# x1's product into the down accumulator moved to unit 26 of the attention, and the scaling of x1's rows moved from VectorE to ScalarE

## The chip, the cores and the metric

The kernel runs on one core of one Trainium2 chip. A core has TensorE (PE, matrix products into PSUM), VectorE (DVE), ScalarE (ACT), GpSimd (POOL) and SyncE (SP, which issues DMAs). The metric is the device time of one execution in microseconds.

## The reference, cut to what matters

```python
xn  = _layernorm(x)                        # x is (8, 512, 128): eight batch rows
s   = attention_1(xn, Wq, Wk, Wv, Wo, ...) # causal, weights 1 - tanh(energy)^2
h   = rmsnorm(xn, norm1_w)
ctx = softmax_attention(h @ wq, h @ wk, h @ wv)
X   = xn + ctx @ wo                        # x1 in the kernel
h2  = rmsnorm(X, norm2_w)
combine = top-2 of 8 experts by softmax(h2 @ router_w)
moe = swiglu(h2, shared) + sum_e combine[:, e] * swiglu(h2, expert e)
out = x + s * silu(X + moe)
```

`X + moe` is the sum that one PSUM accumulator collects: nine down products (the shared expert and eight routed ones) and x1 itself.

## The kernel before, in words

The eight batch rows are done one after another by an order written out by hand, and `row(u, it, following)` stands in each engine's program for one of them. Engines meet at counting semaphores alone, and each engine works strictly through its own program, so whatever stands behind a wait on an engine stands still with it. A row takes about 131 us. It has three parts.

**Units 0 to 15** (N1 = 16) are the softmax attention of the feed-forward block: TensorE makes scores into the PSUM tiles S0 and S1 (L1112), ScalarE takes their exponential into a slot of the tile PT (`weights`, L613), and TensorE multiplies it with V (`with_v`, L1139). VectorE spends most of this part on maxima over score blocks of 512 columns (`maximum`, L758).

**Units 16 to 27** are the second attention. ScalarE writes a sigmoid (L613 again), and VectorE turns it into weights (`weigh`, L813, two halves for each unit). Beside the units stand named pieces of work, given by the table PLACES: at 23 "proj2", behind which VectorE adds the projection to x1 (L857); at 25 "Q1", which ScalarE copies out of PSUM twice (`projection`, L572 and L573); at 26 "h2T", the transpose of the scaled rows (L1048 on TensorE; L586 and L587 on ScalarE, which write h2T and h2hi); at 27 "logits" (L1246) and "K1".

On ScalarE the order around the change is: the halves of unit 24; four squares of x1's rows with their sums (L635); both halves of unit 25; `acc_out`, the copy of the accumulator O0 out of PSUM (L602); Q1's two copies; both halves of unit 26; h2T and h2hi; unit 27. On VectorE, after the first half of unit 24: the inverse root of the mean squares, a chain of eleven tiny steps (L930 to L742); then the four scalings of x1's rows into h2t (L933); then the second half of unit 24 and so on, h2lo (L937) in unit 26, and behind unit 27 the router. On TensorE unit 26 is: first scores, `with_v` of unit 23, second scores, transposes of h2t; unit 27: first scores, `with_v` of unit 24, logits, second scores, K1. In the last row there is no Q1 and no K1, since these belong to the row that follows, and the logits stand behind the second scores.

**The expert part**: for e = 0 to 8 TensorE makes the gate and up products (`expert`, L1172 to L1174), ScalarE takes Silu (L646), VectorE multiplies (L951), GpSimd multiplies by the routing weight (L494; the last expert's by VectorE, L964), and TensorE adds the down product of expert e - 2 into the accumulator O0 (`second_product`, L1156). O0 is the same PSUM tile that one pair of head groups of the second attention uses until `acc_out` reads it in unit 25. Behind expert 8 TensorE does, in this order: the first scores of the next row, the down product of expert 7, the maxima's transpose, more scores, two score blocks for maxima (L1080), then x1's product, four times 128 by 128 by the identity (L1325), and the down product of expert 8. Then VectorE reads O0 (`out_by_s`, L885), ScalarE takes Tanh (L662), VectorE finishes silu (L890), and the next row goes on.

The semaphore down_done counts the products into O0: DOWNS = NE + 1 = 10 for each row, x1's own among them. ScalarE waits for it before it overwrites slots of PT, GpSimd before it overwrites x1 (L498), VectorE before it reads O0 (L883).

Of the kernel before, what the change touches and what calls it, by code (L numbers as in the profile page):

```python
# [140 lines left out]
S_USES = UNITS + NE  # L141
O_USES = (3, 2)
WEIGHED = 2 * len(STAGE2)
DOWNS = NE + 1
DEPTH = 3
SPLIT_STEPS = 8
STORED = 3 * 2 * 16
# [2 lines left out]
def program(nc, x, par, n1w, n2w, w1, w2, router, w_gu, w_dn, out):  # L150
# [4 lines left out]
    with ctx_:  # L155
# [3 lines left out]
        def sem(name):  # L159
            return ctx_.enter_context(nc.semaphore(name))  # L160
# [103 lines left out]
        routed_last = sem("routed_last")  # L264
        down_done = sem("down_done")
        xn_ready, h_ready, h2_ready, h2r_ready = (sem(n) for n in ("xn_ready", "h_ready", "h2_ready", "h2r_ready"))
        squared = sem("squared")
        exps_ready, gap_ready, top_ready, comb_ready = (sem(n) for n in ("exps_ready", "gap_ready", "top_ready", "comb_ready"))
        second_part, parts_ready, prod_ready = sem("second_part"), sem("parts_ready"), sem("prod_ready")
        max_ready = {run: sem("max_ready" + run) for run in RUNS}  # L270
# [262 lines left out]
        def _(act):  # L533
# [63 lines left out]
            def acc_out(it, P):  # L597

                k, _c = acc_use(it, P)
                last = 2 * NT * (P + 1) if P < 2 else N1 + 6 * (P - 1)  # L600
                act.wait_ge(pv_done, it * UNITS + last + SLOTS)
                a.activation(OS[:, P % 2, :], O[k][:, :], ACT.Copy).then_inc(o_read[k], 1)  # L602

            def weights(it, n, q):
                w = width(n)
                if q == 0:
                    act.wait_ge(pv_done, it * UNITS + n + 1)
                done = {0: 0, 1: 1, 2: DEPTH}
                if q == 0 and n in done and it * DOWNS + done[n] > 0:
                    act.wait_ge(down_done, it * DOWNS + done[n])  # L610
                k, c = score_use(it, 2 * n + q)
                act.wait_ge(s_full[k], c + 1)
                a.activation(PT[:, n % SLOTS, 2 * q * w:2 * q * w + 2 * w].rearrange("p (r n) -> p r n", r=2),  # L613
                             S[k][:, :].rearrange("p (r n) -> p r n", r=2)[:, :, 0:w],
                             ACT.Exp if n < N1 else ACT.Sigmoid).then_inc(s_read[k], 1)

            def row(u, it, following):
                bt = it + 1
                outs = {2 * NT + 2: 0, 4 * NT + 1: 1, N1 + 9: 2}
                for n in range(2, UNITS):  # L620
                    names = u.places[n]
                    weights(it, n, 0)
                    for name in names[:len(names) // 2]:
                        take(u, name, bt)
                    weights(it, n, 1)
                    if outs.get(n) == 2:
                        act.wait_ge(*full(u, ("oT2", 1)))
                    if n in outs:
                        acc_out(it, outs[n])
                    for name in names[len(names) // 2:]:  # L630
                        take(u, name, bt)
                    if n == 24:
                        act.wait_ge(*read(u, "proj2"))
                        for t in range(NT):
                            a.activation(h2t[:, t, :], x1[:, t, :], ACT.Square, accum_out=ssum[:, t:t + 1]).then_inc(squared, 1)  # L635
                act.wait_ge(*read(u, "logits"))
                a.activation(lp[:, :, :], ld[:, :, :], ACT.Sigmoid).then_inc(exps_ready, 1)
                a.activation(lq[:, :, :], ld[:, :, :], ACT.Sigmoid, scale=-1.0).then_inc(exps_ready, 1)

                for e in range(NE):  # L640
                    k, c = score_use(it, 2 * (EXPERT + e))
                    act.wait_ge(s_full[k], c + 1)
                    act.wait_ge(down_done, it * DOWNS + e + 1)
                    if e < DEPTH:
                        act.wait_ge(pv_done, it * UNITS + UNITS + e + 1)
                    a.activation(AB[e % DEPTH], S[k][:, :], ACT.Silu).then_inc(s_read[k], 1)  # L646
                    if e == 0:
                        acc_out(it, 3)
                    for name in u.places[EXPERT + e]:
                        take(u, name, bt)  # L650
                    if e == 0:
                        act.wait_ge(gap_ready, it + 1)
                        a.activation(wgap[:, :], dtop[:, :], ACT.Tanh, scale=0.5).then_inc(top_ready, 1)
                if following:
                    a.activation(warm[:, :], n1s[:, :], ACT.Exp)
                    for q in range(2):
                        weights(it + 1, 0, q)
                    take(u, "maxT_W", bt)
                    for q in range(2):
                        weights(it + 1, 1, q)  # L660
                act.wait_ge(out_scaled, it + 1)
                a.activation(gT[:, :], O[0][:, :], ACT.Tanh, scale=0.5).then_inc(o_read[0], 1)  # L662
# [45 lines left out]
        def _(dve):  # L708
# [196 lines left out]
            def row(u, it, following):  # L905
# [17 lines left out]
                for n in range(N1, UNITS):  # L923
                    weigh(it, n, 0)
                    for name in u.places[n]:
                        if name != "logits":
                            take(u, it, name)
                    if n == 24:
                        dve.wait_ge(squared, (it + 1) * NT)
                        step(v.tensor_scalar(root[:, 2, :], ssum[:, :], 1.0 / D, 1e-6, ALU.mult, ALU.add))  # L930
                        inverse_root(rinv[:, 2, :], root[:, 2, :], newton[:, 0, :])
                        for t in range(NT):
                            last = v.tensor_scalar(h2t[:, t, :], x1[:, t, :], rinv[:, 2, t:t + 1], None, ALU.mult)  # L933
                        last.then_inc(h2_ready, 1)
                    if n == 26:
                        dve.wait_ge(*read(u, "h2T"))
                        v.tensor_tensor(h2lo[:, :], h2T[:, :], h2hi[:, :], ALU.subtract).then_inc(h2r_ready, 1)  # L937
                    weigh(it, n, 1)
# [90 lines left out]
        def _(pe):  # L1029
# [88 lines left out]
            def with_v(it, n, half=None):  # L1118
# [25 lines left out]
                if half != 0:  # L1144
                    last.then_inc(pv_done, 1)

            def second_product(it, e):

                if e == 0:
                    pe.wait_ge(o_read[0], it * O_USES[0] + 3)  # L1150
                    k, c = score_use(it, 2 * EXPERT + 1)
                    pe.wait_ge(s_read[k], c + 2)
                else:
                    pe.wait_ge(*((routed, it * (E - 1) + e) if e < NE - 1 else (routed_last, it + 1)))
                for f in range(NFH):
                    last = t_.matmul(O[0][:, :], wdn[:, e, f, :], AB[e % DEPTH][:, f * 512:f * 512 + 512],  # L1156
                                     start=(e == 0 and f == 0), stop=(e == NE - 1 and f == NFH - 1))
                    if f == 0:
                        yield
                last.then_inc(down_done, 1)  # L1160
                yield
# [115 lines left out]
            def row(u, it, following):  # L1277
# [3 lines left out]
                for n in range(2, UNITS):  # L1281
                    if n == N1 - 1:
                        pe.wait_ge(setup, 2)
                    for run, (p0, _p1) in RUNS.items():
                        if n == NT * (p0 // 2) and n:
                            pe.wait_ge(row_in[run], (it + 1) * 64)
                    if n == N1:
                        for name in ("Q1", "K1"):
                            pe.wait_ge(stacked[name], (it + 1) * 32)
                    names = u.places[n]  # L1290
                    for i in range(4):
                        if i % 2 == 0:
                            scores(it, n, i // 2)
                        elif v_at.get(n, N1) < N1 and v_at[n] % NT > 0:
                            with_v(it, v_at[n], i // 2)
                        elif n in v_at and i == 1:
                            with_v(it, v_at[n])
                        if n >= N1:
                            now = names[len(names) * i // 4:len(names) * (i + 1) // 4]
                        else:  # L1300
                            now = {0: names[:2], 2: names[2:]}.get(i, [])
                        for name in now:
                            work(u, it, name)
                with_v(it, UNITS - 3)
# [13 lines left out]
                if following:  # L1318
# [2 lines left out]
                        scores(it + 1, 1, q)  # L1321
                    for name in ROWS[it + 1].places[0]:
                        work(ROWS[it + 1], it + 1, name)
                for t in range(NT):
                    last = t_.matmul(O[0][:, t * 128:t * 128 + 128], x1[:, t, :], ident[:, :], start=False, stop=False)  # L1325
                last.then_inc(down_done, 1)
                for _step in second_product(it, NE - 1):
                    pass
                if not following:
# [63 lines left out]
```

## Time and profile before

| what | value |
|---|---|
| median of 3 runs | 1099.15 us (1097.03, 1099.39, 1099.15) |
| profiled execution, its own time | 1097.14 us |
| its span in the trace | 1095.4 us |
| PE, DVE, ACT, POOL busy | 90%, 76%, 59%, 32% of the span |
| granted TensorE clock, mean | 0.982 |

How to read it: the profile is of one execution. "Busy" counts matmuls whose ends are modelled, so busy time on PE isn't PE at its peak. The chain of waits follows the work back from the last instruction, at each step to what released it, and is the view that tells what a microsecond is worth; the timeline gives starts and durations on each engine. In both, the first two columns are the start and the length in us from the span's start.

### The profile page before, as it was taken

To read this page: it belongs to the slowest core of one execution; us is meant where nothing else is said; L and a number is where in the kernel's file an instruction comes from. 1 tells how busy PE (TensorE), PEld (TensorE's weight loads), DVE (VectorE), ACT (ScalarE), POOL (GpSimd) and SP (SyncE) were. 2 spreads that over 40 slices of the span, in tenths; PEclk is the share of its full clock that TensorE was granted. 3 is DMA by queue.
4 is the path that set the end of the run, shared out by engine and by line. 5 is a ranking of instruction groups with operands and counts; after the bars stand their busy time and mean duration, and the time that the engine had idled before them with its cause. 6 is when DMAs were issued, how large, how long until landed. Compare 5 with 4: busy or idle time off the path is not lost.

```text
span 1095.4 us, 18252 instructions
## 1 busy us (share of the span) xinstructions
PE 990.9 (90%) x6763; PEld 467.3 (43%) x6784; DVE 831.4 (76%) x1684; ACT 646.8 (59%) x882; POOL 351.2 (32%) x211
## 2 busy tenths in 40 slices
PE   4489999899998999889998999989999899988997
PEld 1123464245542455324652346523554245532464
DVE  6885977869776888759878598795977779773962
ACT  3569724786258842698336972379624785258731
POOL 4702443033520355105530154203352033610032
PEclk9589999999999999999999999999999999999999
DMA  7350561023700435105331055211471033600020
GB/s 231 71 109 22 111 169 34 21 55 80 190 20 12 99 93 132 30 2 130 112 83 30 2 130 143 51 31 30 101 181 24 21 79 83 163 20 2 1 79 10
DMA packets 60392, 81.83 MB, mean 75 GB/s; under 512 B 8560, under 2 KB 47728, under 8 KB 57296
## 3 DMA queue, kind: packets, MB, share of 16 engines
q1 hardware_dynamic: 56544, 75.61, 28.3%
q10 hardware_dynamic: 3760, 5.05, 1.4%
q8 instruction: 55, 0.90, 0.4%
q14 instruction: 33, 0.27, 0.1%
HBM read 52.98 MB, written 27.39 MB: 73 GB/s over the span
## 4 chain that ended last, share of the span: by engine, by line
PE 53%; DVE 25%; ACT 12%; issue 4%; DMA 2%; SPq 1%; ACTq 0%; POOL 0%; DVEq 0%; POOLq 0%
PE O L1156 11%; DVE nmax L758 10%; DVE PT L813 9%; PE O L1139 7%; ACT PT L613 7%; PE S L1172 6%; PE S L1174 5%; PE S L1173 5%; PE S L1112 4%; PE M L1075 3%; PE M L1054 2%; PE M L1080 1%; PE O L1075 1%; SPq L368 1%; DMA stackQ<-mTZ 1%
## 5 line engine op out<-in xcount | busy, mean ns | idle before, releaser
L613 ACT ACTIVATE PT<-S 128x1024 f32<-128x1024 f32 (+1 forms) x448 | 417.0, 967 | 113.7 <-PE S L1112 108.7
L813 DVE SCALAR_TENSOR_TENSOR PT<-PT 128x768 f32<-128x768 f32 (+1 forms) x192 | 213.4, 1163 | 101.0 <-ACT PT L613 101.0
L758 DVE TENSOR_REDUCE nmax<-M 128x1 f32<-128x512 f32 x329 | 218.2, 684 | 43.2 <-PE M L1075 28.3
L1139 PE MATMUL O<-PT,V 128*32 128x256 f32 (+3 forms) x2816 | 246.5, 430 | 0.0
L494 POOL TENSOR_TENSOR PT<-PT,CB 128x1024 f32<-128x1024 f32 x56 | 133.6, 2392 | 261.2 <-DVE PT L951 146.9
L646 ACT ACTIVATE PT<-S 128x1024 f32<-128x1024 f32 x72 | 73.9, 1027 | 241.4 <-PE S L1174 241.4
L479 POOL TENSOR_TENSOR split<-split,parts 128x512 f32<-128x512 f32 x30 | 90.9, 3029 | 372.0 <-ACT parts L573 372.0
L1112 PE MATMUL S<-stackQ,stackK 64*128 64x512 bf16 (+3 forms) x1024 | 166.3, 347 | 9.5 <-DMA stackQ<-mTZ 5.3
L758 DVE TENSOR_REDUCE nmax<-O 128x1 f32<-128x512 f32 x183 | 125.1, 684 | 36.5 <-PE O L1075 17.6
L1172 PE MATMUL S<-h2hi,wgu_hi 128*128 128x512 f32 x288 | 148.7, 516 | 4.3 <-DVE PT L951 4.2
L1156 PE MATMUL O<-PT,wdn 128*128 128x512 f32 x288 | 142.9, 595 | 0.9
L1174 PE MATMUL S<-h2hi,wgu_lo 128*128 128x512 f32 x288 | 113.6, 395 | 0.0
L1173 PE MATMUL S<-h2lo,wgu_hi 128*128 128x512 f32 x288 | 112.9, 392 | 0.0
L951 DVE TENSOR_TENSOR PT<-PT,S 128x1024 f32<-128x1024 f32 x72 | 87.2, 1212 | 20.5 <-PE S L1174 19.8
L1112 PEld LDWEIGHTS S<-stackQ,stackK 64*128 64x128 bf16 x1024 | 43.5, 93 | 138.8 <-issue 74.6
L1139 PEld LDWEIGHTS O<-PT,V 128*32 128x32 f32 x2816 | 57.6, 108 | 73.3 <-issue 69.6
L1080 PE MATMUL M<-stackK,stackQ 48*128 48x512 bf16 x189 | 59.6, 411 | 19.7 <-DVE nmax L758 10.2
L1172 PEld LDWEIGHTS S<-h2hi,wgu_hi 128*128 128x128 f32 x288 | 55.3, 192 | 39.0 <-issue 28.4
L1156 PEld LDWEIGHTS O<-PT,wdn 128*128 128x128 f32 x288 | 53.3, 191 | 32.9 <-issue 29.4
L1106 PE MATMUL S<-never,identb 128*128 128x128 bf16 (+1 forms) x384 | 60.7, 240 | 6.9 <-ACT PT L613 6.6
L1080 PE MATMUL O<-stackK,stackQ 48*128 48x512 bf16 x99 | 40.4, 408 | 21.5 <-issue 9.7
L1174 PEld LDWEIGHTS S<-h2hi,wgu_lo 128*128 128x128 f32 x288 | 54.0, 188 | 12.4
(198 smaller groups left out, 1044.5 us busy)
## 6 DMA issues: line engine op xcount, KB each, us to landing
CB<-scrC SPq DMA_DIRECT2D x64, 256.0 KB, 5.6
stackQ<-scrQ SPq DMA_DIRECT2D x30, 384.0 KB, 5.5
stackK<-scrK SPq DMA_DIRECT2D x30, 384.0 KB, 6.3
scrQ<-parts SPq DMA_DIRECT2D x32, 192.0 KB, 3.3
scrK<-parts SPq DMA_DIRECT2D x30, 192.0 KB, 5.9
scrQ<-parts SPq DMA_DIRECT2D x32, 128.0 KB, 3.4
scrK<-parts SPq DMA_DIRECT2D x30, 128.0 KB, 5.2
KX<-scrK SPq DMA_DIRECT2D x14, 192.0 KB, 3.4
```

Of the source, the lines that this page charges most:

```text
L479: g.tensor_tensor(s[:, :], s[:, :], p[:, 0, :], ALU.subtract).then_inc(pool_step, 1)
L494: g.tensor_tensor(a, a, w, ALU.mult).then_inc(routed, 1)
L613: a.activation(PT[:, n % SLOTS, 2 * q * w:2 * q * w + 2 * w].rearrange("p (r n) -> p r n", r=2), S[k][:, :].rearrange("p (r n) -> p r n", ...
L758: v.tensor_reduce(nmax[:, h % 2, h // 2, t:t + 1], M[k][:, :], AX.X, ALU.max, negate=True).then_inc(m_read[k], 1)
L813: v.scalar_tensor_tensor(p, p, 1.0, p, ALU.subtract, ALU.mult).then_inc(weighed, 1)
L1080: t_.matmul(M[k][:, :], stack["Q2"][rows, hp, t * 128:t * 128 + 128], stack["K2"][rows, hp, :], start=True, stop=True).then_inc(m_full[k], 1)
L1112: last = t_.matmul(S[k][:, 512 * r + at:512 * r + at + L - i0], stack[key][rows, hp, 128 * j:128 * j + 128], stack[query][rows, hp, i0:L], ...
L1139: last = t_.matmul(O[k][32 * q:32 * q + VW, i0:i1], V[:, j, 4 * g + q, :], PT[:, n % SLOTS, w * q + at:w * q + at + i1 - i0], start=(j == ...
L1156: last = t_.matmul(O[0][:, :], wdn[:, e, f, :], AB[e % DEPTH][:, f * 512:f * 512 + 512], start=(e == 0 and f == 0), stop=(e == NE - 1 and ...
L1172: t_.matmul(dst, wgu_hi[:, e, cols], h2hi[:, :], start=True, stop=False)
L1173: t_.matmul(dst, wgu_hi[:, e, cols], h2lo[:, :], start=False, stop=False)
L1174: last = t_.matmul(dst, wgu_lo[:, e, cols], h2hi[:, :], start=False, stop=True)
```

## The change

x1's product is taken out from between the last two down products. It becomes `x_turned`, called in unit 26 of the second attention, behind the second scores and ahead of the transposes of h2t. It opens the accumulation in O0 with a product whose moving operand is a part of the tile KX that holds zeros (64 by 512, bf16), and adds the four products of x1's rows. The down products no longer open or interrupt the accumulation, and down_done counts nine for each row. The four scalings of x1's rows by the inverse root move from VectorE to ScalarE, behind the copy of O0 in unit 25 and ahead of Q1's copies; VectorE tells ScalarE through a new semaphore, `rooted`.

```diff
-DOWNS = NE + 1
+DOWNS = NE
...
-        squared = sem("squared")
+        squared, rooted = sem("squared"), sem("rooted")
...
@@ scalar, weights()
-                done = {0: 0, 1: 1, 2: DEPTH}
-                if q == 0 and n in done and it * DOWNS + done[n] > 0:
+                done = {0: 1, 1: 2, 2: DEPTH}
+                if q == 0 and n in done:
                     act.wait_ge(down_done, it * DOWNS + done[n])
@@ scalar, row()
                     if n in outs:
                         acc_out(it, outs[n])
+                    if n == 25:
+                        act.wait_ge(rooted, it + 1)
+                        for t in range(NT):
+                            last = a.activation(h2t[:, t, :], x1[:, t, :], ACT.Copy, scale=rinv[:, 2, t:t + 1])
+                        last.then_inc(h2_ready, 1)
                     for name in names[len(names) // 2:]:
                         take(u, name, bt)
@@ vector, row()
                         inverse_root(rinv[:, 2, :], root[:, 2, :], newton[:, 0, :])
-                        for t in range(NT):
-                            last = v.tensor_scalar(h2t[:, t, :], x1[:, t, :], rinv[:, 2, t:t + 1], None, ALU.mult)
-                        last.then_inc(h2_ready, 1)
+                        dve.sem_inc(rooted, 1)
@@ tensor
+            def x_turned(u, it):
+
+                pe.wait_ge(*read(u, "proj2"))
+                pe.wait_ge(o_read[0], it * O_USES[0] + 3)
+                pe.wait_ge(kset, 4)
+                t_.matmul(O[0][:, :], identb[HALF:128, :], KX[HALF:128, 0, 0, :], start=True, stop=False)
+                for t in range(NT):
+                    t_.matmul(O[0][:, t * 128:t * 128 + 128], x1[:, t, :], ident[:, :], start=False, stop=False)
+
             def second_product(it, e):
 
                 if e == 0:
-                    pe.wait_ge(o_read[0], it * O_USES[0] + 3)
                     k, c = score_use(it, 2 * EXPERT + 1)
                     pe.wait_ge(s_read[k], c + 2)
...
-                                     start=(e == 0 and f == 0), stop=(e == NE - 1 and f == NFH - 1))
+                                     start=False, stop=(e == NE - 1 and f == NFH - 1))
@@ tensor, row(), the attention's units
+                        if n == 26 and i == 3:
+                            x_turned(u, it)
                         for name in now:
                             work(u, it, name)
@@ tensor, row(), behind the experts
-                for t in range(NT):
-                    last = t_.matmul(O[0][:, t * 128:t * 128 + 128], x1[:, t, :], ident[:, :], start=False, stop=False)
-                last.then_inc(down_done, 1)
                 for _step in second_product(it, NE - 1):
                     pass
```

## Rows read from the trace of the kernel before

**Rows 1.** The page: busy time by engine, and the chain that ended last

```profile
PE 990.9 (90%) x6763; PEld 467.3 (43%) x6784; DVE 831.4 (76%) x1684; ACT 646.8 (59%) x882; POOL 351.2 (32%) x211
PE 53%; DVE 25%; ACT 12%; issue 4%; DMA 2%; SPq 1%; ACTq 0%; POOL 0%; DVEq 0%; POOLq 0%
```

**Rows 2.** The chain of waits from 574 to 581 us, the end of a row

```profile
574.67 1.91 PE O L1156 x4
...
577.59 1.09 PE O L1325 x8
578.67 1.73 PE O L1156 x4
...
580.43 0.69 DVE sT L885
```

**Rows 3.** The timeline of DVE from 574 to 581.5 us; brackets: idle before, releaser

```profile
575.30 1.22 DVE L964 TENSOR_TENSOR PT<-PT,CB 128x1024 f32<-128x1024 f32 x1
577.60 1.29 DVE L758 TENSOR_REDUCE nmax<-M 128x1 f32<-128x512 f32 x2 [1.09 <-PE M L1080]
```

**Rows 4.** The chain of waits from 500 to 535 us, units 24 to 27

```profile
510.19 0.61 DVE x L857
...
517.38 0.74 ACT h2hi L587
...
518.17 1.06 PE M L1246 x8
```

**Rows 5.** The timeline from 503 to 532 us, ScalarE and VectorE's rows of unit 25

```profile
511.42 0.29 ACT L635 ACTIVATE h2t<-x 128x128 f32<-128x128 f32 x1
...
511.71 0.29 ACT L635 ACTIVATE h2t<-x 128x128 f32<-128x128 f32 x1
...
514.29 0.69 ACT L572 ACTIVATE split<-M,qs 128x512 f32<-128x512 f32 x1
...
514.61 0.16 DVE L742 SCALAR_TENSOR_TENSOR rinv<-newton,rinv 128x4 f32<-128x4 f32 x1
514.81 0.87 DVE L933 TENSOR_SCALAR h2t<-x,rinv 128x128 f32<-128x128 f32 x4
514.86 0.70 ACT L573 ACTIVATE parts<-M,qs 128x512 bf16<-128x512 f32 x1
```

**Rows 6.** Line L613: duration min/median/max in ns, and the forms

```profile
L613 ACT ACTIVATE PT<-S x448: 804/1024/1081, 52.6 to 1038.2; 128x1024 f32<-128x1024 f32 x106, 128x768 f32<-128x768 f32 x44
```

**Rows 7.** The timeline of PE from 514 to 519.5 us

```profile
514.55 0.34 PE L1112 MATMUL S<-stackQ,stackK 64*128 64x384 bf16 x2
515.74 0.66 PE L1048 MATMUL M<-ident,h2t 128*128 128x128 f32 x4 [0.86 <-DVE h2t L933]
...
518.17 1.06 PE L1246 MATMUL M<-rts,h2T 128*128 128x8 f32 x8 [0.40 <-ACT h2hi L587]
```

**Rows 8.** Stretches: length, busy PE, PEld, DVE, ACT, POOL; clock, DMA share, GB/s

```profile
510.80:518.20 7.40, 5.88 (x53) 2.14 (x49) 6.98 (x21) 7.38 (x18) 2.46 (x1) 1.00 0.79 203
...
518.20:577.50 59.30, 58.68 (x269) 34.52 (x272) 47.57 (x94) 20.73 (x30) 27.91 (x13) 1.00 0.37 96
```

**Rows 9.** The chain of waits from 1056 to 1096 us, the last row's end

```profile
1086.57 0.89 PE O L1325 x8
```

**Rows 10.** The timeline from 1026 to 1044 us, the last row

```profile
1034.48 1.52 ACT L613 ACTIVATE PT<-S 128x768 f32<-128x768 f32 x2
...
1034.71 0.87 DVE L933 TENSOR_SCALAR h2t<-x,rinv 128x128 f32<-128x128 f32 x4
...
1036.92 0.68 ACT L587 ACTIVATE h2hi<-M,n2s 128x512 fp32r<-128x512 f32 x1
...
1040.24 0.19 PEld L1172 LDWEIGHTS S<-h2hi,wgu_hi 128*128 128x128 f32 x1 [1.00 <-DVE h2lo L937]
```

**Rows 11.** The timeline of PE from 1049 to 1061 us, the last row

```profile
1052.58 0.50 PE L1172 MATMUL S<-h2hi,wgu_hi 128*128 128x512 f32 x1 [0.68 <-DVE PT L951]
...
1058.77 1.98 PE L1156 MATMUL O<-PT,wdn 128*128 128x512 f32 x4
```

## The prediction

> **What bounds the kernel now.** I read the page first, then the chain of waits, then the timeline at the two places that the change touches. The page says that TensorE is busy 90% of the span, and the chain gives it 53%, VectorE 25% and ScalarE 12% [rows 1]. So no engine bounds the whole, and each place has to be asked for itself.
>
> At the end of a row the chain runs on TensorE: scores for the maxima, x1's product for 1.09 us, the last down product for 1.73 us, then VectorE's read of the accumulator [rows 2]. Nothing else is late there. What the last down product waits for besides, VectorE's weighing of expert 8, is over at 575.30 + 1.22 = 576.52, a microsecond before x1's product begins, and VectorE's two maxima end at 577.60 + 1.29 = 578.89, 1.5 us before it can read the accumulator [rows 3].
>
> In units 24 to 27 the chain runs on ScalarE. From the first square, just behind x1's sum, which ends at 510.19 + 0.61 = 510.80, it stays there until h2hi ends at 518.12 [rows 4], with ScalarE busy for 7.38 of 7.40 us [rows 8], and TensorE's logits start at 518.17, after an idle 0.40 us that ends with h2hi [rows 7]. Behind them TensorE is busy 58.68 of 59.30 us to the end of the row [rows 8], so what the logits lose the row loses. VectorE's scalings are not on that chain. TensorE does wait for them, 0.86 us [rows 7], but ScalarE reads the transposes only later, behind Q1's copies and unit 26, so they cost nothing where they stand.
>
> **The change part by part.**
>
> *x1's product at the row's end, removed.* The chain gives it 1.09 us. But the down product behind it would now follow other work. The same four matmuls take 1.91 us where they follow scores and 1.73 us where they follow x1's product [rows 2]: 0.18 us of loading weights comes back. I take 1.09 - 0.18 = 0.91 us, with 1.09 as the other end. In the last row, where the product stood between down products, it cost 0.89 us [rows 9], and I take that. VectorE's read then starts at about 579.5, still behind its maxima at 578.89; 0.6 us of cover is left, so nothing new holds it. The other members of the row's start (Tanh on ScalarE, x1's refill on GpSimd) wait for the same product and move with it, and SP's queue is not touched: the change issues no DMA. Sum: 7 x 0.91 + 0.89 = 7.3 us less.
>
> *x_turned in unit 26.* TensorE has nothing to do from the second scores' end at 514.89 to 515.74 [rows 7]. Into that go the product of zeros and four products. No row shows the product of zeros. Its nearest row is a pair of score matmuls, 0.34 us [rows 7], and I take 0.2 to 0.4 us; the four cost the 1.09 us of before. TensorE is through by 516.4, and with the transposes' 0.66 us by 517.0. ScalarE will want them only at 518.5 (below). Cost zero, hidden under ScalarE with 1.5 us to spare; if that cover were gone, up to 0.6 us for each row. Its waits are met: proj2 was read before x1 was written, and the copy of O0 ends by 514.4.
>
> *The scalings, off VectorE.* They took 0.87 us for four [rows 5]. VectorE gets this back in each row, ahead of unit 24's second half. It isn't on the chain there, so the gain is nothing in rows 0 to 6.
>
> *The scalings, onto ScalarE.* This is the term that decides. ScalarE was to begin Q1's copy at 514.29 [rows 5]. Now it first waits for `rooted`. The inverse root ends at 514.77, and VectorE's next instruction began at 514.81 [rows 5]; with the semaphore's way to the other engine I take 514.88. So 0.59 us goes by waiting. Then come four scalings of 128 x 128 with a scale read from memory. Two squares of this size start 0.29 us apart, with a read of the accumulator in each but no such scale; two copies of 512 columns with such a scale start 0.57 us apart [rows 5], and by the slope of L613, (1024 - 804) / 256 = 0.86 ns for an element [rows 6], 384 elements fewer make it 0.24 us. I take 0.28 us, near the squares, which also read SBUF. The ends are 0.11 us (128 elements by that slope and nothing besides) and 0.40 us (the square's duration of 0.29 us and the 0.12 us by which a copy's duration, 0.69 us, exceeds its spacing, 0.57 us: no overlap at all). Four make 1.12 us, and Q1's copy starts at 516.00, 1.71 us late. Queued behind it on ScalarE, without a gap anywhere [rows 8], are Q1's copies, unit 26, h2T, h2hi and unit 27. So h2hi and the logits are 1.7 us late, and unit 27's first scores, which wait for unit 26's read, too. GpSimd's split of Q1 starts as late, no later than the rest of the row. VectorE reaches h2lo about when h2hi is ready, 0.3 us later than before, and so has more room behind TensorE than it had. For seven rows: 7 x 1.71 = 12.0 us more.
>
> The Trainium skill, ScalarE: Activation LUTs, "Rules for kernel authors", puts multiplications on VectorE and not on ScalarE, which speaks against this change. "What ACT_TABLE_LOAD costs" on that page gives an ACTIVATE 186 ns plus 0.833 ns for an element, 93 ns more for a scale by pointer, and 93 ns of overlap. The trace agrees on the square: 0.29 us against 186 + 107 ns. By that page the four would be 293 ns apart, and the sum an estimated 0.4 us higher.
>
> *The last row* has no Q1 copy and its chain runs on VectorE, through the scalings [rows 10]; removing 0.87 us there would be a gain. But TensorE, which waited for h2lo until 1040.24, is next. ScalarE starts unit 26 at 1034.75 + 1.12 = 1035.9 instead of 1034.5, h2hi ends near 1038.6 instead of 1037.6, the logits and a product with V (2.1 us) follow, and the experts start near 1040.9, 0.65 us late. TensorE's waits behind that are 0.68 us for VectorE and 0.2 us for GpSimd's weighing [rows 11]. The delay fits inside them: I take -0.2 us, between -0.8 and +0.3.
>
> **Sum.** 12.0 - 7.3 - 0.2 = +4.5 us against the profiled execution's own 1097.14 us (span 1095.4): 1101.6 us. The runs shown lie in two pairs, this one and 1097.03 below, 1099.15 and 1099.39 above; against the median of 1099.15 the sum is 1103.7. I put the forecast between: 1102.5 us. A measurement of this kernel can tell about 0.2%, 2.2 us, from no change.
>
> **The rivals.**
>
> *A: TensorE's gain stays, ScalarE's loss doesn't show.* The place is the logits' wait for h2hi. If something else releases them, or ScalarE has idle time there that the chain hides, the shift is absorbed and 7.3 + 0.2 us are won: 1097.14 - 7.5 = 1089.6, or 1091.6 on the median. It decides for faster below a shift of 0.75 us; with 0.59 us waited, four scalings would have to take 0.04 us each. For it: ScalarE is busy 59% overall. Against it: between 511 and 518 us ScalarE is busy throughout, and the idle time on TensorE ends with h2hi [rows 7, 8]. 11%.
>
> *B: both terms are kind.* Scalings 0.20 us apart, halfway to the lower end, make a shift of 1.39 us, and x1's product is worth its full 1.09 us: 7 x 0.30 - 0.9 - 0.2 = +1.0 us. At both ends (0.11 us, so a shift of 1.03, and 1.09 us) it is 7 x -0.06 - 1.1 = -1.5 us. Both are within 0.2%. For it: no row shows a scaling by itself. 19%.
>
> *C: scalings don't overlap.* At 0.40 us the shift is 2.19 us: 7 x 1.28 - 1.1 = +7.9 us, 1105.0 us on the profiled execution. It shares the sign with the forecast. 10%.
>
> *D: x_turned is not hidden.* It delays the transposes past 518.5 only if it takes 2.9 us, more than twice its price. Inside the forecast's chance.
>
> The forecast itself has 60%. Slower by over 0.2% is forecast and C, 70%; within 0.2% is B, 19%; faster is A, 11%. The range leaves out A and C's far end: 1097.0 (B, between the pairs, less its lower end) to 1107.0 (C, between the pairs, 1106.1, and a little for x_turned).
>
> **What would show it.** Right: the idle time of ScalarE for `rooted` (0.4 us, eight times), four scalings under 0.3 us apart, Q1's copy starts 3.5 + 1.7 = 5.2 us behind the end of x1's sum and the logits 7.4 + 1.7 = 9.1 us behind it; x_turned inside what was TensorE's idle time, ended before h2hi; at the row's end no L1325, the last down product 1.9 us long, a row longer by 0.8 us. Wrong: logits less than 8.4 us behind x1's sum (then A or B), a row's end that gives up clearly more or less than 0.9 us, or a new wait there, of VectorE for its maxima.

## The result and the profile after

The changed kernel is slower: 1110.7 us against 1099.27 us (medians of four runs each), ratio 1.0108, 95% interval 1.009 to 1.0126. Its four runs are 1105.48, 1109.64, 1111.77 and 1113.09 us, so they spread over 7.6 us where the kernel before spreads over 4.3. The profiled execution is the fastest of them, 1105.48 us with a span of 1103.7. I had forecast 1102.5 us, in a range up to 1107.0.

The chain of waits in units 24 to 27, the same stage as [rows 4], in the changed kernel (start, length, what; DVEq is VectorE's sequencer):

```profile
512.18 0.60 DVE x L862
...
516.82 0.03 DVEq L937
...
521.14 0.71 ACT h2hi L587
...
521.90 1.25 PE M L1257 x8
```

x1's sum ends at 512.78. `rooted` comes 4.07 us behind it, Q1's copy 5.3 us (3.5 before) and the logits 9.12 us (7.37 before), so the logits are 1.75 us late. The chain now passes through VectorE's inverse root into ScalarE's scalings.

ScalarE's and TensorE's timelines of that stage, beside [rows 5] and [rows 7]. First ScalarE:

```profile
516.87 1.28 ACT L633 ACTIVATE h2t<-x,rinv 128x128 f32<-128x128 f32 x4 [0.47 <-DVEq L937]
518.05 0.67 ACT L572 ACTIVATE split<-M,qs 128x512 f32<-128x512 f32 x1
```

Then TensorE:

```profile
516.72 0.38 PE L1155 MATMUL O<-KX,identb 64*128 64x512 bf16 x1
517.03 1.16 PE L1157 MATMUL O<-ident,x 128*128 128x128 f32 x8
518.20 0.66 PE L1051 MATMUL M<-ident,h2t 128*128 128x128 f32 x4
520.05 0.39 PE L1109 MATMUL S<-never,identb 128*128 128x256 bf16 x2 [1.19 <-ACT PT L613]
...
521.90 1.25 PE L1257 MATMUL M<-rts,h2T 128*128 128x8 f32 x8 [0.41 <-ACT h2hi L587]
...
523.96 2.07 PE L1057 MATMUL M<-xnT,w1s 128*128 128x512 f32 x2
```

The product of zeros and x1's four products fill what was TensorE's wait for h2t. A new wait of 1.19 us has come behind the transposes, for ScalarE's late reading of unit 26's scores. That wait stands in each of the seven rows ahead of the last. And in this row, from about 522.6 us on, the same matmuls last nearly twice as long: K1's two take 2.07 us where they take 1.12 us in other rows. The stretches of that kernel (length, busy PE, PEld, DVE, ACT, POOL, granted clock, DMA share, GB/s):

```profile
516.00:522.00 6.00, 4.39 (x48) 2.32 (x40) 5.73 (x9) 5.53 (x12) 2.35 (x2) 1.00 0.93 183
522.90:529.70 6.80, 6.80 (x25) 2.04 (x28) 6.04 (x18) 3.53 (x6) 1.38 (x1) 0.52 0.02 5
529.70:586.00 56.30, 55.67 (x246) 33.01 (x241) 41.08 (x77) 18.10 (x24) 20.05 (x10) 1.00 0.35 95
```

Why this row and not another stays open. The row before it has the same stretch, figure for figure, and keeps its clock; so do five more rows with the same waits:

```profile
384.37:390.37 6.00, 4.39 (x48) 2.32 (x40) 5.73 (x9) 5.53 (x12) 2.35 (x2) 1.00 0.93 184
```

The end of a row, the chain of waits, beside [rows 2]:

```profile
449.71 1.93 PE O L1167 x4
...
584.38 1.93 PE O L1167 x4
...
716.74 1.93 PE O L1167 x4
...
848.34 1.93 PE O L1167 x4
```

The last down product takes 1.93 us, where x1's product and it took 1.09 + 1.73 = 2.82: 0.89 us saved, as forecast (0.91). The distance of these marks is the length of a row: 131.60 us for the last pair, and 134.67 us from 449.71 to 584.38, the row with the fall. Before, the matching rows took 130.76 and 131.12 us. So a plain row is 0.84 us longer (forecast 0.80) and the one with the fall 3.55 us; the fall costs 2.7 us by this reckoning.

### The profile page after: what moved, and what is told of

It reads as the page before. It is cut to its first block, busy times and chain, and to the rows that moved or that the text cites. A ratio compares the mean times of both kernels' runs of the same rounds, so it can differ in the third digit from the quotient of the medians.

```text
span 1103.7 us, 18276 instructions
## 1 busy us (share of the span) xinstructions
PE 998.1 (90%) x6771; PEld 468.8 (42%) x6792; DVE 839.5 (76%) x1652; ACT 656.2 (59%) x914; POOL 311.3 (28%) x211
## 4 chain that ended last, share of the span: by engine, by line
PE 54%; DVE 26%; ACT 11%; issue 4%; DMA 3%; SPq 1%; ACTq 0%; POOL 0%; DVEq 0%; POOLq 0%
PE O L1167 12%; DVE nmax L763 10%; DVE PT L818 10%; PE O L1142 7%; PE S L1183 6%; PE S L1185 6%; ACT PT L613 6%; PE S L1184 6%; PE S L1115 4%; PE M L1078 3%; PE M L1057 2%; PE M L1083 1%; PE O L1078 1%; SPq L368 1%; DMA stackQ<-mTZ 1%
## 5 line engine op out<-in xcount | busy, mean ns | idle before, releaser
L613 ACT ACTIVATE PT<-S 128x1024 f32<-128x1024 f32 (+1 forms) x448 | 416.6, 965 | 113.7 <-PE S L1115 108.6
L818 DVE SCALAR_TENSOR_TENSOR PT<-PT 128x768 f32<-128x768 f32 (+1 forms) x192 | 227.0, 1234 | 102.7 <-ACT PT L613 100.8
L479 POOL TENSOR_TENSOR split<-split,parts 128x512 f32<-128x512 f32 x30 | 46.1, 1537 | 384.1 <-ACT parts L573 384.1
L1083 PE MATMUL M<-stackK,stackQ 48*128 48x512 bf16 x189 | 59.6, 411 | 19.7 <-DVE nmax L763 10.2
L1109 PEld LDWEIGHTS S<-never,identb 128*128 128x128 bf16 x384 | 27.3, 99 | 81.5 <-ACT PT L613 58.9
L1185 PEld LDWEIGHTS S<-h2hi,wgu_lo 128*128 128x128 f32 x288 | 54.2, 188 | 12.5
```

What stands on the lines that cost most here:

```text
L818: v.scalar_tensor_tensor(p, p, 1.0, p, ALU.subtract, ALU.mult).then_inc(weighed, 1)
L1109: t_.matmul(S[k][:, 512 * r:512 * r + 128 * len(js)].rearrange("p (j n) -> p j n", n=128), identb[:, :], mask, start=True, stop=False, ski ...
L1185: last = t_.matmul(dst, wgu_lo[:, e, cols], h2hi[:, :], start=False, stop=True)
```

## The experiments

The theory after the result: ScalarE's queue costs the 1.7 us for each row that I had counted, and what is above the sum is TensorE's clock, which falls in a varying number of rows behind a wait that has grown. The rival: the excess comes from x1's product in its new place, or from something outside TensorE. For each run the text gives the median and the ratio to the kernel before, and "row" is the mean of five rows between the same marks of the chain. For the kernel before that is (970.41 - 315.66) / 5 = 130.95 us, from the starts of x1's product in its chain of waits:

```profile
315.66 1.09 PE O L1325 x8
...
970.41 1.09 PE O L1325 x8
```

**The product alone.** The scalings go back to VectorE.

```diff
-                    if n == 25:
-                        act.wait_ge(rooted, it + 1)
...
-                        dve.sem_inc(rooted, 1)
+                        for t in range(NT):
+                            last = v.tensor_scalar(h2t[:, t, :], x1[:, t, :], rinv[:, 2, t:t + 1], None, ALU.mult)
+                        last.then_inc(h2_ready, 1)
```

> The changed kernel with the four scalings back on VectorE; x1's product stays in unit 26. Theory 1 (ScalarE's queue is what is paid for, and TensorE's clock falls in unit 27 where it has waited too long for it): the row's end gives back 0.91 us in seven rows and 0.89 in the last, the transposes end at most 0.1 us behind the moment at which ScalarE wants them, so 6.4 to 7.3 us less than the kernel before, about 1091 us against 1098, and no execution with more clock falls than before has. Rival (the product's new place itself costs, by its waits or by the product of zeros): as slow as the kernel before or slower.

Measured 1090.21 us, ratio 0.9927 (0.9903 to 0.9951): faster than both kernels. The chain's marks of a row's end:

```profile
314.45 1.93 PE O L1164 x4
...
964.49 1.93 PE O L1164 x4
```

(964.49 - 314.45) / 5 = 130.01 us for a row, 0.94 less than before. TensorE's timeline in unit 26 and ahead of the logits:

```profile
511.73 0.38 PE L1152 MATMUL O<-KX,identb 64*128 64x512 bf16 x1
512.03 1.16 PE L1154 MATMUL O<-ident,x 128*128 128x128 f32 x8
513.03 0.60 PE L1048 MATMUL M<-ident,h2t 128*128 128x128 f32 x4
...
515.17 1.06 PE L1254 MATMUL M<-rts,h2T 128*128 128x8 f32 x8 [0.26 <-ACT h2hi L587]
```

x1's sum ends at 507.80 in this row, so the logits stand 7.37 us behind it, as before: the place is free in these seven rows, and the rival that the place costs has fallen for them. (The last row is another case; see below.)

**The scalings alone.** x1's product stays between the last down products.

```diff
                     if n in outs:
                         acc_out(it, outs[n])
+                    if n == 25:
+                        act.wait_ge(rooted, it + 1)
+                        for t in range(NT):
+                            last = a.activation(h2t[:, t, :], x1[:, t, :], ACT.Copy, scale=rinv[:, 2, t:t + 1])
+                        last.then_inc(h2_ready, 1)
...
-                        for t in range(NT):
-                            last = v.tensor_scalar(h2t[:, t, :], x1[:, t, :], rinv[:, 2, t:t + 1], None, ALU.mult)
-                        last.then_inc(h2_ready, 1)
+                        dve.sem_inc(rooted, 1)
```

> The kernel before with the four scalings on ScalarE alone; x1's product stays between the last down products. Theory 1: logits 1.74 us late in seven rows, 12.2 us, nothing from the last row to -0.9, and on top of it falls of TensorE's clock in a varying number of rows at about 2.7 us each, more than in the changed kernel, since here no x1 product fills TensorE's wait: 1110 to 1125 us, clocks under 0.98. Rival (the excess over the sum of the queue's delay comes from x1's product in its new place): 1110 us, all runs within 2 us, clocks at the kernel before's 0.982.

Measured 1136.35 us, ratio 1.0352 (1.0319 to 1.0384), clocks 0.950 to 0.955: in the direction of the theory, and beyond its numbers. A row takes (1006.46 - 323.93) / 5 = 136.51 us, 5.56 more than before.

```profile
323.93 1.09 PE O L1328 x8
...
1006.46 1.09 PE O L1328 x8
```

TensorE's timeline shows both waits and the slow clock behind them:

```profile
529.75 0.66 PE L1051 MATMUL M<-ident,h2t 128*128 128x128 f32 x4 [1.32 <-ACT h2t L633]
531.60 0.61 PE L1109 MATMUL S<-never,identb 128*128 128x256 bf16 x2 [1.19 <-ACT PT L613]
```

Without x1's product in it, the first wait is 1.32 us and comes on top of the second. The clock falls in each of the first seven rows, here already at 531.6, and stays low longer, 6.8 to 10.2 us. An eighth fall, of 3.4 us, comes elsewhere, at 630 us in the softmax attention, behind a wait of 1.69 us for a DMA. I had priced a fall at 2.7 us; here a row loses 5.56 - 1.75 = 3.8 us to its clock.

**Filling the waits of that kernel.** Nine products of zeros for each row are added to it, four ahead of the transposes and five behind.

```diff
+            def zeros(count):
+
+                for _k in range(count):
+                    t_.matmul(O[0][:, :], identb[HALF:128, :], KX[HALF:128, 0, 0, :], start=True, stop=True)
...
+                        if n == 26 and i == 3:
+                            pe.wait_ge(o_read[0], it * O_USES[0] + 3)
+                            zeros(4)
                         for name in now:
                             work(u, it, name)
+                        if n == 26 and i == 3:
+                            zeros(5)
```

> The run with the scalings alone on ScalarE (x1's product between the last down products), and besides nine products of zeros on TensorE in unit 26, four ahead of the transposes of h2t and five behind them, in its waits of 1.32 and 1.19 us; nothing reads their result. Theory 1 (of that run's 38 us over the kernel before, ScalarE's queue makes 12 and the clock that falls in every row the rest): 1108 to 1112 us, clocks at 0.977 or above, so about 25 us less for nine products more. Rival (the 38 us are ScalarE's and VectorE's, and the clock is slow because the engine is idle, not the other way round): 1133 us or more, whatever TensorE does in its waits.

Measured 1110.88 us, ratio 1.0117 (1.01 to 1.0134), all four runs between 1110.49 and 1111.60, clocks 0.980 to 0.982. TensorE's timeline and the marks in the chain:

```profile
519.45 1.02 PE L1153 MATMUL O<-KX,identb 64*128 64x512 bf16 x4
520.92 0.66 PE L1051 MATMUL M<-ident,h2t 128*128 128x128 f32 x4 [0.46 <-ACT h2t L633]
521.51 1.25 PE L1153 MATMUL O<-KX,identb 64*128 64x512 bf16 x5
...
524.62 1.06 PE L1254 MATMUL M<-rts,h2T 128*128 128x8 f32 x8 [0.40 <-ACT h2hi L587]
```

```profile
319.01 1.09 PE O L1338 x8
...
982.19 1.09 PE O L1338 x8
```

A row takes (982.19 - 319.01) / 5 = 132.64 us, 1.69 more than before: the queue's term by itself, forecast 1.71. No row of the profile has a fall. The nine products do nothing but occupy the array, and they save 25.3 us: this run is 12.5 us above the kernel before, the one without them 37.7, each against the kernel before on its own chip. That separates the two costs of the scalings: 12.5 us for ScalarE's queue and 25.3 us for the clock. The rival, that the clock is low merely because there is little to do, has fallen.

**Filling the changed kernel's wait.** Five products of zeros behind the transposes, where it waits 1.19 us.

```diff
                         for name in now:
                             work(u, it, name)
+                        if n == 26 and i == 3:
+                            for _k in range(5):
+                                t_.matmul(O[0][:, :], identb[HALF:128, :], KX[HALF:128, 0, 0, :], start=False, stop=False)
```

> The changed kernel with five more products of zeros (64 by 512, bf16) behind the transposes in unit 26, in what is TensorE's 1.19 us wait for ScalarE; they add nothing to the accumulator. Theory 1 (the runs at 1110 to 1113 us are those in which TensorE's clock fell in two to four rows behind this wait): more work and less time, 1101 to 1104 us in all runs, clocks at 0.982, no half-speed stretch behind the first 62 us. Rival (the excess over the sum is a delay of something else: a DMA, GpSimd, another chip): 1105 to 1113 us as the changed kernel, or more by what the five products delay.

Measured 1103.77 us, ratio 1.0047 (1.0032 to 1.0062), nine runs between 1102.82 and 1105.54. A row takes 131.78 us by the marks of its chain, 0.83 more than before (forecast 0.80 by the sum).

```profile
319.79 1.93 PE O L1167 x4
...
978.71 1.93 PE O L1167 x4
```

The clocks are 0.979 to 0.984 rather than 0.982 throughout. The profiled run, with 0.979, has no fall in any row; its low stretch at the start is 44.4 us long, where that of the kernel before is 37.6. So this kernel is what my sum described.

**The changed kernel again**, on the chip that ran the kernel with nine products of zeros. (The one with five ran on another chip, contrary to the text below; the kernel before had medians of 1098.41 and 1098.62 us on the two.)

> The changed kernel once more, on the chip of the fillers. Theory 1: times spread over 1101 to 1113 us in steps of about 3 us with the number of clock falls (clock 0.982 at the fast end, 0.971 at the slow one), median some 5 us above the 1103.8 of its kin with five products of zeros. Rival (its first runs were on another, slower chip): 1102 to 1105 us.

Measured 1111.71 us, ratio 1.012 (1.0103 to 1.0137), four runs from 1110.08 to 1112.86. So it isn't the chip: beside the kernel before the ratio is that of its first runs (1.0108), and over twice as far from 1 as that of the kernel with five products of zeros (1.0047). The spread was smaller than I expected. The clocks, 0.971 to 0.974, suggest several falls in each of the four runs, but only one was profiled. The chain's marks in its profiled run, clock 0.971:

```profile
188.56 1.93 PE O L1167 x4
...
321.67 1.93 PE O L1167 x4
...
454.88 1.93 PE O L1167 x4
...
587.99 1.93 PE O L1167 x4
...
723.49 1.93 PE O L1167 x4
...
855.09 1.93 PE O L1167 x4
```

The rows are 133.11, 133.21, 133.11, 135.50 and 131.60 us. The first four hold a fall each. A short one, in the stretch of 3.5 us below, costs 1.5 us against the plain row of 131.60. The one of 6.8 us costs 3.1 us: without a fall, in the first profile, the same row took 716.74 - 584.38 = 132.36 us. Together they are 7.6 us.

```profile
262.10:265.60 3.50, 3.50 (x15) 0.84 (x14) 3.50 (x4) 1.60 (x3) 1.39 (x2) 0.58 0.00 0
```

**The scalings behind Q1's copies.** They stay on ScalarE, but it doesn't stand idle for `rooted`.

```diff
                         acc_out(it, outs[n])
+                    for name in names[len(names) // 2:]:
+                        take(u, name, bt)
                     if n == 25:
                         act.wait_ge(rooted, it + 1)
...
                         last.then_inc(h2_ready, 1)
-                    for name in names[len(names) // 2:]:
-                        take(u, name, bt)
```

> The changed kernel with ScalarE's four scalings behind Q1's two copies instead of ahead of them, so that it does not sit idle for the inverse root. Theory 1: the logits are late by four scalings alone, 4 x 0.295 = 1.18 us, and a row costs 1.18 - 0.91 = 0.27 us: 7 x 0.27 - 1.3 = +0.6 us against the kernel before, plus clock falls; 4 us less than the changed kernel without its clock falls. Rival (the scalings' own time is what counts and the wait for rooted is hidden elsewhere): as slow as the changed kernel.

Measured 1100.03 us, ratio 1.0016 (1.0 to 1.0032), ten runs, clocks 0.977 to 0.982. A row takes 131.23 us, 0.28 more than before (forecast 0.27).

```profile
318.22 1.93 PE O L1167 x4
...
974.35 1.93 PE O L1167 x4
```

TensorE waits 0.57 us ahead of the transposes and 0.40 us ahead of the logits here, and no row of the profile has a fall. The order of two pieces of work on ScalarE is worth some 11 us of the changed kernel's time: 0.56 us for each row, 3.9 us, and the falls.

**The product behind the transposes**, with the scalings on VectorE.

```diff
-                        if n == 26 and i == 3:
-                            x_turned(u, it)
                         for name in now:
                             work(u, it, name)
+                        if n == 26 and i == 3:
+                            x_turned(u, it)
```

> The kernel with x1's product alone moved (scalings on VectorE), but the product stands behind the transposes of h2t instead of ahead of them. Theory 1 (the new place costs nothing because it lies in TensorE's wait for h2t; behind the transposes only the 0.26 to 0.40 us ahead of the logits are free): the logits come 0.9 us later in seven rows, so the gain is given back, 1090.2 + 6 = 1096 to 1097 us. Rival (any place in unit 26 does, since ScalarE is what the stage waits for): 1090 us again.

Measured 1098.21 us, ratio 0.9997 (0.9986 to 1.0008). A row takes (971.92 - 317.42) / 5 = 130.90 us, 0.89 more than with the product ahead. Its TensorE timeline has the old wait again and none ahead of the logits:

```profile
516.57 0.66 PE L1048 MATMUL M<-ident,h2t 128*128 128x128 f32 x4 [0.86 <-DVE h2t L933]
517.15 0.39 PE L1152 MATMUL O<-KX,identb 64*128 64x512 bf16 x1
517.47 1.16 PE L1154 MATMUL O<-ident,x 128*128 128x128 f32 x8
```

The gain needs that one wait of 0.86 us as its cover; behind the transposes, 0.66 us of work later, it is gone. The time came out 1 to 2 us above what I expected, about which the rows say nothing more.

**A filler in the kernel before.** Three products of zeros ahead of the transposes.

```diff
+                        if n == 26 and i == 3:
+                            pe.wait_ge(o_read[0], it * O_USES[0] + 3)
+                            zeros(3)
```

> The kernel before with three products of zeros ahead of the transposes of h2t in unit 26, in TensorE's wait of 0.86 us. If some of its executions at 1099 to 1101 us have a fall of the clock inside a row, these are gone: 1096 to 1098.5 us in all runs. If the spread comes from the start, where the clock is low for 34 to 44 us in the profiles, nothing changes: 1096 to 1101 us, clocks 0.977 to 0.983. I expect the second.

Measured 1097.25 us, ratio 0.9993 (0.9984 to 1.0003). No run is above 1098.8, where the kernel before has some up to 1101.6, but the interval holds no change, so this is inconclusive: whether the kernel before has a fall inside a row in its slower executions stays open. Its profiled run (clock 0.978) has its low stretch at the start alone.

## Why the prediction was wrong

*x1's product at the row's end* was right: 0.91 us forecast, 0.89 read, 0.94 us for each row in the run that moves the product alone (rival B's full 1.09 us didn't come). So was the cover behind it; no new wait came at the row's end.

*x_turned costs nothing* was right in rows 0 to 6, in its place ahead of the transposes, as the run with the product alone shows. The product of zeros is 0.38 us long, and the next one starts 0.31 us behind it.

*The scalings on ScalarE* were right in size: waiting for `rooted` until 4.09 us behind x1's sum (4.08 forecast), scalings 0.295 us apart (0.28 forecast), Q1's copy at 5.3 us, the logits 1.75 us late (1.71). The estimate worked out from the Trainium skill, ScalarE: Activation LUTs, "What ACT_TABLE_LOAD costs", was 0.293 us, and the trace bears it out. A plain row is 0.84 us longer where I had 0.80.

*The last row* was off by little. I had it 0.2 us shorter besides x1's product; from one read of O0 to the next it became 0.38 us shorter in all, and 0.89 of that is the product, so the rest cost 0.5 us. Its experts did start late by about the 0.65 us forecast (0.54), but TensorE's waits behind it did not take that up. Part of this is x_turned, which isn't hidden in this row: TensorE's wait was only 0.56 us there before, and the chain of the changed kernel runs through the five products:

```profile
1043.76 0.22 PE O L1155
1043.98 1.09 PE O L1157 x8
```

With the product alone moved the row is 0.72 us shorter, so the place costs some 0.2 us of the 0.5.

*The step that failed* is the end of the scalings' term: "So h2hi and the logits are 1.7 us late", times seven, and nothing else. I asked whose work a late h2hi holds up and didn't ask what the longer wait does to TensorE itself. I even noted that x_turned fits "what was TensorE's idle time" and took that for a cost of zero, although 1.19 us of new idle time came behind it. The missing term is the fall of the clock: 1.5 to 3.1 us in each row that has one, four rows in one profiled execution (7.6 us together) and one in the other. It makes the difference between the 1103.8 us of the filled kernel, which my sum describes, and the 1110.7 to 1111.7 us of the changed one. The granted clock of 0.982 that I read for the kernel before held no warning by itself. Nor does the length of one wait tell: the kernel before has longer ones than 1.19 us in the softmax attention, and its clock doesn't fall there.

```profile
609.63 0.39 PE L1112 MATMUL S<-stackQ,stackK 64*128 64x512 bf16 x2 [1.33 <-ACT PT L613]
```

By the Trainium skill, TensorE: Matmul & The Clock Gate, Part 1, an active array is granted 2.4 GHz and an idle one 1.2 GHz. The trace agrees on the two levels and the direction, but the array was far from idle ahead of the fall: it was busy for 4.39 of 6.00 us. No row ahead of the change showed how near to a fall this stage stood; the experiments did.

Of the rivals, A (the loss doesn't show) is refuted by the 1.75 us and B (both terms kind) by the 0.295 and 0.89 us; C had the right side for another reason, since the scalings do overlap; D (x_turned not hidden) didn't come in rows 0 to 6.

## What to carry to other kernels

Price a wait that grows on TensorE twice: once for what stands behind it, and once for the clock, as a risk with a range, since equal rows of one execution kept the clock and lost it. A handful of products of zeros in the wait is a cheap test: if more work makes the kernel faster, the clock was part of the price. And when a change has two halves, run each alone: here one half gains 0.7%, and the other costs 3.5% by itself and turns the sum.

## What the runs showed of the hardware that I had not expected

TensorE's clock fell in unit 26 with no single wait longer than 1.32 us: 1.19 and 0.41 us in the changed kernel, in one and in four of seven rows; 1.32 and 1.19 us with the scalings alone, in each of seven rows. Products of zeros count as activity for it: with nine for each row the falls of the latter are gone, with five those of the former.

GpSimd and VectorE get in each other's way, and in the three kernels below a shift of one or two microseconds turned around who paid. GpSimd's first split step of Q1 took up to 8.19 us in the kernel before, where it began as VectorE began a run of four weighings. In the changed kernel, where it begins 2.4 us later against that run (519.47 behind 516.92 us, before 515.74 behind 515.60), none takes over 2.14 us. First the kernel before, then the changed one:

```profile
L479 POOL TENSOR_TENSOR split<-split,parts x30: 1154/1171/8189, 46.3 to 933.0; 128x512 f32<-128x512 f32 x30
```

```profile
L479 POOL TENSOR_TENSOR split<-split,parts x30: 1152/1168/2141, 46.1 to 942.5; 128x512 f32<-128x512 f32 x30
```

VectorE paid instead: its four weighings last 5.06 us where they lasted 4.09, and its h2lo 1.52 us where it lasted 0.68. With the scalings behind Q1's copies, GpSimd begins 0.81 us behind the run; its step takes 1.16 us and VectorE's four weighings 6.86. In the rows read, at 516 to 524 us, none of this was on the chain.

```profile
521.91 1.52 DVE L940 TENSOR_TENSOR h2lo<-h2T,h2hi 128x512 fp32r<-128x512 f32 x1
```
